# A relational graph network: 24000 of 100000 edges leave the gather and are counted into 128-square blocks

## The reference

```
deg = edges per dst;  dis = deg > 0 ? 1/sqrt(deg) : 0
h   = x @ W0
X1  = layernorm(x + segment_sum(h[src] * dis[src] * dis[dst], dst))
X   = X1;  inv_deg = 1 / (edges with the same dst and type)
for l in 0..3:
    h   = X @ weights[l][r]  for r in 0..3
    agg = segment_sum(h[etype, src] * inv_deg, dst)
    out = agg + X @ root[l] + bias[l]
    X   = elu(layernorm(out) * gamma[l] + beta[l]) + X
return layernorm(X1 + X)
```

## Time and profile before

| | us |
|---|---|
| median of three runs | 5888.52 |
| profiled execution: time | 5888.28 |
| profiled execution: span | 5886.5 |
| busy in the span: PE / DVE / POOL / ACT | 4383.9 / 4219.3 / 4257.3 / 1468.0 |
| chain that ended last: PE / issue / DVE | 56% / 20% / 16% |

### The profile page before, as it was taken

The page is one execution under the profiler, slowest core; times in us unless marked ns, Lnnn a source line. Parts: engine busy times, 40 slices in busy tenths (PEclk is TensorE's granted clock), DMA queues, the critical chain, the costliest instruction groups (busy, mean ns, idle before and its releaser), DMA issues.

```text
span 5886.5 us, 69627 instructions
## 1 busy us (share of the span) xinstructions
PE 4383.9 (74%) x16659; PEld 2236.8 (38%) x16659; DVE 4219.3 (72%) x10916; ACT 1468.0 (25%) x3865; POOL 4257.3 (72%) x4345
## 2 busy tenths in 40 slices
PE   2888577777777777777777778777777776777676
PEld 1444333333334444443344444343443433333332
DVE  8888788888876666665666666566666656767765
ACT  1666655555531111111111111111111110000000
POOL 0888677777757777776777777677777767777776
PEclk7999899999999999999999999899999999999999
DMA  1000344444444444444444434444444443333334
GB/s 48 1 1 1 108 119 122 120 120 119 117 127 116 116 120 119 117 119 113 116 116 120 120 116 120 112 116 116 120 119 117 119 104 105 106 105 106 106 105 108
DMA packets 280592, 617.40 MB, mean 105 GB/s; under 512 B 77007, under 2 KB 150561, under 8 KB 280152
## 3 DMA queue, kind: packets, MB, share of 16 engines
q0 software_dynamic: 203040, 529.13, 32.9%
q1 hardware_dynamic: 77240, 84.68, 4.3%
HBM read 549.83 MB, written 63.36 MB: 104 GB/s over the span
## 4 chain that ended last, share of the span: by engine, by line
PE 56%; issue 20%; DVE 16%; ACT 4%; DVEq 2%; DMA 1%; SPq 0%; ACTq 0%
PE bank L533 35%; PE bank L535 9%; DVE arena L977 6%; PE bank L490 6%; DVE emat L952 3%; PE bank L564 3%; ACT emat L691 2%; DVE arena L888 2%; DVE arena L901 1%; PE bank L503 1%; PE bank L500 1%; DVEq L962 1%; ACT hout L682 1%; DVE found L969 1%; DVEq L977 1%
## 5 line engine op out<-in xcount | busy, mean ns | idle before, releaser
L425 POOL DMA_INDIRECT msg<-h_table,g_rel x2580 | 2442.9, 947 | 872.8 <-PE bank L533 590.3
L533 PE MATMUL bank<-msg,emat 128*128 128x256 f32 x6452 | 2145.0, 415 | 993.9 <-issue 536.1
L977 DVE TENSOR_TENSOR arena<-arena,bank 128x256 f32 x4030 | 1686.1, 418 | 1209.6 <-PE bank L533 1162.7
L533 PEld LDWEIGHTS bank<-msg,emat 128*128 128x128 f32 x6452 | 1039.6, 192 | 2329.5 <-DVE emat L952 1407.7
L535 PE MATMUL bank<-zeros 128*128 128x512 f16 x4030 | 1548.3, 384 | 0.0
L952 DVE TENSOR_SCALAR emat<-iota,node,weight 128x128 f32<-128x128 f32 x3224 | 1218.6, 380 | 184.9 <-DVE arena L977 69.6
L425 POOL DMA_INDIRECT msg<-h_table,g_src x646 | 620.4, 960 | 224.0 <-issue 110.6
L425 POOL DMA_INDIRECT hout<-h_table,g_rel x644 | 610.0, 947 | 221.8 <-PE bank L533 145.9
L533 PE MATMUL bank<-hout,emat 128*128 128x256 f32 x1608 | 530.1, 412 | 247.3 <-issue 124.4
L969 DVE SCALAR_TENSOR_TENSOR found<-iota,key,arena 128x512 f16<-128x512 f32 x806 | 605.2, 751 | 132.9 <-issue 20.7
L408 POOL DMA_INDIRECT placed_dram<-leaving,idx x300 | 427.5, 1425 | 232.0 <-issue 225.0
(11 more groups left out here) (154 smaller groups left out, 2331.0 us busy)
## 6 DMA issues: line engine op xcount, KB each, us to landing
h_table<-hout SPq DMA_DIRECT2D x100, 512.0 KB
msg<-h_table,g_rel POOLq DMA_INDIRECT x2580, 2.8
msg<-h_table,g_src POOLq DMA_INDIRECT x646, 2.8
hout<-h_table,g_rel POOLq DMA_INDIRECT x644, 2.8
arena<-inv_dram SPq DMA_DIRECT2D x1, 6400.0 KB, 20.0
placed_dram<-leaving,idx POOLq DMA_INDIRECT x300
w_sb<-in_L_gnn_weights_dram SPq DMA_DIRECT2D x8, 512.0 KB, 5.3
h_table<-hout SPq DMA_DIRECT2D x25, 128.0 KB, 1.7
```

What stands on the lines that cost most here:

```text
L425: pool.indirect_dma_start(out=slots[n % RING], out_offset=None, in_=table[:, :], in_offset=bass.IndirectOffsetOnAxis(ap=rows[:, t:t + 1], ...
L533: pe.matmul(agg_ps[n % NPS][:, 0:D], emat[:, n % BODY, :], slots[n % RING], start=True, stop=True).then_inc(s_mm, 1)
L977: dve.tensor_tensor(a, a, agg_ps[n % NPS][:, 0:D], ALU.add).then_inc(s_acc, 1)
```

## The change

The six chunks of 128 source nodes that are used most are found on the chip. Of the edges whose source lies in one of them, the first 24000 (`NDE`) are "dense"; they get window numbers above 24 (three of the chunks each, `H` = 2 halves of `KH` = 3), so they are sorted into blocks of their own behind the 618 tiles that are left (`NT`) for the gathers; 238 tiles (`DT`) are for them.

Between sort and stage 0, `build_counts` turns each of the 50 blocks (window x half) into counts: for each dense tile PE multiplies a one-hot of sources (384 columns) with a one-hot of type and node (512 columns), summed in PSUM over the block's tiles, in two sets of three banks whose addresses come from registers. ACT converts finished counts to int16 and stores them in HBM.

In every stage the tables' rows of the six chunks are loaded into SBUF (`hcache`, `load_cache`), ACT loads and converts the counts of each window (`convert`), PE does 24 products per window into banks 4 and 5, spread over the tiles (`dense_tile`), and DVE adds them into `acc` (`dense_added`), scaled in layers 1 to 4 by the inverse counts per type. `NPS` goes from 5 to 3, `HALF` from 16 to 8 (matrices 8 tiles ahead), `found` from two buffers to one, and the filler has 256 columns of a number row instead of 512 zeros. The ring keeps 20 slots.

```diff
+    KH, H = 3, 2
+    K = KH * H
+    NDE = E * K // NW
+    NT = (E - NDE + NW * (P - 1)) // P
+    DT = (NDE + NW * H * (P - 1)) // P
-    HALF = 16
+    HALF = 8
-    NPS = 5
+    NPS = 3
+        def dense_tile(j, i):
+            d = done_at[j - 1] if j else 0
+            return d + 4 + i * 16 // (K * R) if j else 14 + i * 7 // (K * R)
...  SP
+            for j in range(CW):
+                sp.wait_ge(s_hw[j], 16 * NC)
+            load_cache(0)
             for q in range(L + 1):
                 if q > 0:
+                    sp.wait_ge(s_hs, (q * NW + ONE0) * 16)
+                    load_cache(q)
...  PE
+            def dense_product(q, j, i):
+                n, (c, r) = q * NW + j, divmod(i, R)
+                m = n * K + c
+                if i == 0:
+                    pe.wait_ge(s_hc, (q + 1) * (16 * K))
+                    if n:
+                        pe.wait_ge(s_dense, n)
+                if r == 0:
+                    pe.wait_ge(s_conv, m + 1)
...
+                mm = pe.matmul(to, blocks[m % AF][:, r * P:(r + 1) * P], rows,
+                               start=(c == 0 and first), stop=(c == K - 1 and last))
+                if r == R - 1:
+                    mm.then_inc(s_used, 1)
...
-                    pe.matmul(spare_ps[:, :], zeros16[:, 0:P], zeros16[:, :], start=True, stop=True)
+                    pe.matmul(spare_ps[:, 0:D], iota16[:, 0:P], iota16[:, 0:D],
+                              start=True, stop=True)
...
+            def build_counts():
...
+                for t in range(DT):
...  three register loads when t % 4 == 0: after (4 values), sets (8), edges (8)
+                    if t:
+                        pe.wait_ge(s_free, after[k])
+                        for c in range(KH):
+                            mm = end_set(bank_at(shut, step, c))
+                            if c == KH - 1:
+                                mm.then_inc(s_built, 1)
+                            begin_set(bank_at(opened, step, c))
+                    pe.wait_ge(s_oh, t + 1)
+                    for c in range(KH):
+                        pe.matmul(cols(psum, at + c * R * P if c else at, R * P),
+                                  src_hot[t % OH][:, c * P:(c + 1) * P], key_hot[t % OH],
+                                  start=False, stop=False)
...  ACT
+            def convert(n, c):
+                m, (h, k) = n * K + c, divmod(c, KH)
+                if k == 0:
+                    act.wait_ge(s_counts[h], (n + 1) * 16)
+                if m >= AF:
+                    act.wait_ge(s_used, m - AF + 1)
+                act.copy(blocks[m % AF], counts[:, h, k * R * P:(k + 1) * R * P]
+                         ).then_inc(s_conv, 1)
+                if k == KH - 1 and n + 1 < (L + 1) * NW:
+                    act.wait_ge(s_conv, m + 1)
+                    load_counts(n + 1, h)
...  in serve_messages, a window's order
                     window_sd(n)
+                    if j + 1 < NW:
+                        for c in range(4):
+                            convert(n + 1, c)
                     window_exp(n - NW)
+                    if j + 1 < NW:
+                        for c in range(4, K):
+                            convert(n + 1, c)
...  DVE
+            totals(s_hi, NW, tot_s)
...  the six chunks are found and marked, their edges numbered; d_hi gets + NW or + 2 NW
+            totals(d_hi, NB, tot)
...  the rank loop runs over NB = 75 for NW = 25
+            for t in range(DT):
+                if t >= OH:
+                    dve.wait_ge(s_built, t - OH + 1)
+                dve.tensor_scalar(src_hot[t % OH], iota16[:, 0:KH * P], d_slot[:, t:t + 1], None,
+                                  ALU.is_equal)
+                dve.tensor_scalar(key_hot[t % OH], iota16[:, 0:R * P], d_key[:, t:t + 1], None,
+                                  ALU.is_equal).then_inc(s_oh, 1)
...
+            def dense_added(q, j):
+                n, v = q * NW + j, window_at(mybir.EngineType.DVE, j)
+                a = cols(acc, v * D, D)
+                dve.wait_ge(s_used, (n + 1) * K)
+                dve.wait_ge(s_acc, ACC0 + q * NT + done_at[j] - 2)
+                if q == 0:
+                    dve.tensor_tensor(a, a, dense_ps[0][:, 0:D], ALU.add).then_inc(s_dense, 1)
+                else:
+                    for r in range(R):
+                        if r:
+                            dve.wait_ge(s_dstep, (n - NW) * (R - 1) + r)
+                        s = dve.scalar_tensor_tensor(
+                            a, dense_ps[r // 2][:, r % 2 * D:(r % 2 + 1) * D],
+                            cols(inv, v + r * NW, 1), a, ALU.mult, ALU.add)
+                        s.then_inc(s_dstep if r < R - 1 else s_dense, 1)
+                dve.wait_ge(s_dense, n + 1)
...
+                    steps[done_at[j] - 2] = lambda j=j: dense_added(q, j)
```

More of the change, by code:

```diff
@@ L543, in _ @@
             for half in range(2):
-                mm = pe.matmul(banks[6 + half][0:1, 0:HB], order_col[:, :],
-                               win_ge[:, half * HB:(half + 1) * HB], start=True, stop=True)
-            mm.then_inc(s_wmm, 1)
+                pe.matmul(banks[6 + half][0:1, 0:WB], order_col[:, :],
+                          win_ge[:, half * WB:(half + 1) * WB], start=True, stop=True)
+            pe.matmul(misc_ps[0:1, 0:DT], ones[0:ND, 0:1], begun_ge, start=True, stop=True
+                      ).then_inc(s_wmm, 1)
             pe.wait_ge(s_hev, BUF + NW)
@@ L575, in _, with begin_set, end_set, bank_at @@
             pe.wait_ge(s_decoded, 1)
+            def begin_set(at):
+                return pe.matmul(cols(psum, at, R * P), zeros16[:, 0:P], zeros16,
+                                 start=True, stop=False)
+            def end_set(at):
+                return pe.matmul(cols(psum, at, 1), zeros16[:, 0:P], zeros16[:, 0:1],
+                                 start=False, stop=True)
+            def bank_at(first, step, c):
+                return nc.s_assert_within(first + step * c if c else first, 0, NOWHERE,
+                                          skip_runtime_bounds_check_because="its set or NOWHERE")
@@ L577, in _ @@
+            build_counts()
+            pe.wait_ge(s_free, ND + 2)
             for q in range(L + 1):
@@ new lines, in _ @@
+            done(dve.tensor_reduce(place[:, :], pair_a, AXX, ALU.add))
+            done(dve.tensor_tensor(pair_a, over_windows(place[:, :]), by_window(iota[:, 0:NW]),
+                                   ALU.is_equal))
+            done(dve.tensor_tensor(pair_b, pair_a, over_windows(iota[:, 0:NW]), ALU.mult))
+            done(dve.tensor_reduce(top[:, :], pair_b, AXX, ALU.add))
+            done(dve.tensor_copy(top_i[:, :], top[0:1, 0:K]))
+            for i in range(K):
+                done(dve.tensor_scalar(hits[2], s_hi, top[0:EP, i:i + 1], float(i + 1),
+                                       ALU.is_equal, ALU.mult))
+                done(dve.tensor_tensor(d_place, d_place, hits[2], ALU.add))
@@ new lines, in _ @@
+            a_d, b_d, c_d, e_d = (v[:, NT:NTA] for v in (a_i, b_i, c_i, e_i))
+            done(dve.scalar_tensor_tensor(d_key[:, :], a_d, float(P), b_d, ALU.mult, ALU.add))
+            done(dve.tensor_scalar(e_d, c_d, P - 1, None, ALU.bitwise_and))
+            done(dve.tensor_copy(d_slot[:, :], e_d))
+            done(dve.tensor_scalar(c_d, c_d, 7, None, ALU.arith_shift_right))
+            chunk, part = e_d.bitcast(f32), a_d.bitcast(f32)
+            done(dve.tensor_copy(chunk, c_d))
+            for i in range(K):
+                if i % KH:
+                    done(dve.tensor_scalar(part, chunk, top[:, i:i + 1], float(i % KH * P),
+                                           ALU.is_equal, ALU.mult))
+                    done(dve.tensor_tensor(d_slot[:, :], d_slot[:, :], part, ALU.add))
```

431 lines of the change are left out of this document (331 added, 100 removed).

## The result

The changed kernel takes 5865.75 us (median of 17 runs, 5860.09 to 5886.32), the kernel before 5890.01 (17 runs): ratio 0.9962, 95% interval 0.9954 to 0.9969. The forecast was 5548 with a range of 5340 to 5830, so it is wrong by 318 us and the time lies outside. A repeat (after_same) gave 0.9972 (0.9959 to 0.9984).

A forecast was written before the change was run, and what follows sets the result against it. POOL's gather rate was taken to bound the layers, DVE's pace stage 0. Start of counting 957, counting 524 + 1, stage 0 830, three layers of 810 and a last of 804 gave 5546 of span, 5548 us; range 5340 to 5830.

The forecast's parts named there:

- What bounds the kernel: In a layer, POOL's gathers at their own 1.252 us spacing plus some 25 us of turn-round; DVE's pace in stage 0.
- The keys: Ahead of the sort, added count, marking, sizes and rank, all serial on DVE: 262 us; counting then starts at 957.
- Counting: In build_counts, 2.2 us per dense tile, nearest to the sequencer's time: 524 us, within 340 and 880.
- the array-paced rival: In counting, the sequencer runs ahead and a tile costs 1.43 us: 183 less, 5365 us in all; chance 0.20.
- The rival of dear loads: In counting, PE's register loads cost 1.25 us per tile for 0.45: +190, 5738 us in all; chance 0.05.
- The layers, 810 each: Layers 1 to 3: gathers and turn-round 798 us, plus 12 us for PE's lag, makes 810 each.
- a little over POOL's 30.9 when it lags at all and under it when it waits for messages: Layers 1 to 3, per window: PE needs 28.5 us plus waits of 0.7, 1.2 and 1.4, 31.8 for POOL's 30.9.
- the 12 us of lag: At the end of layers 1 to 3, time to drain PE's lag: 12 us per layer, between 0 and 85.
- The rival that PE paces the layers: In layers 1 to 3, waits fall whole on PE, 34.2 us per window: +219, 5767 us in all; chance 0.15.
- wrong in kind: Sign of failure: dense adds or ACT's conversion stop a layer over 3 us per window, or counting passes 3.6 per tile.
- Stage 0, 830: Stage 0 from the end of counting: DVE's pace of 1.276 us per tile, 787 us, plus smaller terms: 830 us.
- ACT's conversions (150 x 0.58 = 87) hide beside its 592 busy of 1061 us: In stage 0, ACT's 87 us of conversions were taken as hidden, adding nothing to the 830 us.

The follow-up runs named there:

- best_d: Changed kernel with dense adds spread over four tiles, no filler, a fourth bank and stage 0's first three conversions moved: 5502.10 us, 0.9343; slower chips 0.9346, 0.9305, 0.9297.
- spread_add: Changed kernel with, in layers 1 to 4, one of a window's four dense adds at each of four tiles: 5674.17 us, 0.9632 of the kernel before.
- before_fill256: Kernel before with only its filler cut from 512 to 256 columns, of a number row where there were zeros: 5889.72 us, ratio 0.9998.

## Why the prediction was wrong

- **What bounds the kernel: right.** best_d has the layers (800 to 802) and the last one (805) that POOL's rate and the turn-round give, and the last layer of the changed kernel (807.5 for 804) shows it too: without window products PE has the room.
- **The keys: right.** 950.7 for 957. The rank loop holds 75 scans, 3.04 us apart:
```profile
L1167 DVE TENSOR_TENSOR_SCAN arena<-arena,hout x75: 1864/1870/1884, 168.2 to 393.2; 125x800 f32<-125x800 f32 x75
```
- **Counting: right in size, by luck.** 491 / 238 = 2.06 us for 2.2, for another reason than mine. PE in order of time:
```profile
1147.23 0.81 PE L768 MATMUL psum<-emat 128*128 128x512 f16 x3
...
1148.60 0.81 PE L768 MATMUL psum<-emat 128*128 128x512 f16 x3
...
1149.97 0.81 PE L768 MATMUL psum<-emat 128*128 128x512 f16 x3
1152.98 0.17 PE L730 MATMUL psum<-found 128*128 128x1 f16 x1 [2.21 <-issue]
...
1154.05 1.49 PE L768 MATMUL psum<-emat 128*128 128x512 f16 x3
```
Inside four tiles the array sets the rate, 1.37 us per tile, so the forty register operations that I put at 1.8 us are hidden: the array-paced rival was right there. But at the three register loads, every four tiles, PE often stands for some 2.2 us (over the stage 57 such waits, 90.3 us) and then works for a while at 1.2 GHz (three products in 1.49 us for 0.81): I had the loads' time inside the sequencer's, that rival had it nowhere, and neither had the clock. The rival of dear loads is answered too: their medians are 0.334, 0.591 and 0.589 us and the longest of 180 is 1.15, some 0.38 us per tile for my 0.45 and its 1.25.
- **The layers, 810 each: wrong (888).** The failing step is "a little over POOL's 30.9 when it lags at all and under it when it waits for messages", and the 12 us of lag drawn from it: PE never got back to waiting for messages, and its clock, which the sum took as it was, fell at each stop. The waits themselves I had nearly right in sum. The block of adds has the length I gave it (2.4 us for 2.3) and stops PE for 49.1 / 25 = 2.0 us per window for my 1.2; the conversion stops it for 22.9 / 25 = 0.9 for my 1.4. What stood at nothing is the slower work behind a stop: in layer 2 140 us at half clock lose some 70 by an estimate, 2.8 us per window. PE's own work, 28.5 x 25 = 712 us, with 91 idle and these 70 is 873 of 891; 18 are not told apart. In spread_add the same sum, 712 + 60 + 17, is 789 of 819, so the 712 are likely 20 to 30 too few. The rival that PE paces the layers had 85 us of lag per layer, which should be 82.5 by its own sum; measured were 78 above the forecast, 90 in all. It was right on who sets the pace and near in a layer's time (883 for 884 to 891), but that is in part luck: it had more idle time than there was (5.0 us per window for these two waits, 2.9 measured) and nothing for the clock. I had its chance at 0.15, with the argument that a wait only bites when PE isn't waiting for a message. Of the mark set for "wrong in kind", 3 us per window for one of the two waits, neither came to it.
- **Stage 0, 830: wrong (956).** The failing step is "ACT's conversions (150 x 0.58 = 87) hide beside its 592 busy of 1061 us". Their busy time does, their waits don't: 112 waits for a block, in a fixed order with the matrices, the norm and `half_out`. I reckoned with ACT's share of busy time and not with its order. Moving half of them gave 56 us; the fourth bank and the missing filler 45 (945 to 900); with both, 853 from the end of counting, and the last 23 us are open. The sum also had no term for PE in this stage, only DVE's pace; PE is busy for 817 of the 948 us in the rows above.
- **The trace of before could have warned of the clock.** It had 0.97 with PE 78% busy, and I took it as a constant of the sum. It is an outcome: it is 0.92 or 0.93 in the layers in which PE stopped about once per window, and 0.98 with the same products once spread_add had shortened the stops.

With best_d's edits the layers have the pace that the forecast gave them (5502 us in all for 5548; 40 us of that are the keys and the counting, and best_d has no filler, which the forecast's kernel keeps): the gain was there, and was lost to two waits that the change added and to the slower clock behind them.

## What to carry to other kernels

When work moves onto an engine until it is at 90% of the bound, price each wait that it meets once per period, and what follows it (here 2.9 us of waits per window came with some 2.8 us lost to the half clock), and count in how many buffers the other engine's longest uninterrupted block must be covered: three banks at 0.54 us don't cover 2.4 us, and spreading the same four operations over four tiles gave 199 us. For an engine with a written order, list where each new instruction may have to wait and what stands behind it; its busy share says nothing on that. TensorE's lower clock cost nothing here while another engine set the pace (before_fill256), and was paid on top of each stop when TensorE set it.

## What the hardware showed that I had not expected

- Less work on PE made the kernel slower: cutting the dense products to 16 columns took the granted clock of a layer from 0.86 to 0.64 and the layer from 1007 to 1079 us, on chips of the slower kind.
- The clock can fall without cost: before_fill256 runs its layers at 0.93 for 0.97 in the same time, best_d at 0.94 in the time of POOL's rate.
- Chips differ: 5890 us on some and 6652, 6718 and 6725 on three others for the kernel before, the message stages (1.255 us per gather in best_d, about 1.48 in a layer of best) and not the loops ahead of them (counting starts at 950 to 953 on all). Long straight code alone doesn't explain it: counting is that too, and takes only 3% longer there. More of PE's and DVE's idle time there is marked as waiting for nothing that the profile shows; what it is stays open.
